# Attention with a mixture of experts: VectorE's norm statistics and expert choice move to other steps

## The reference

```
x = x + Attention(layernorm(x), ctx, ctx, mask)     16 heads of 64
    scores = q k^T + mask;  softmax;  probs v;  Wo
x = x + Experts(layernorm(x))
    s = sigmoid(xt gate^T);  the 4 largest of s + gate_b among 16 experts
    w = s of these 4, over their sum, times 2.5
    sum over the chosen e of w_e * (silu(gate_e) * up_e) W2_e^T,  plus one shared expert
```

## Time and profile before

| | us |
|---|---|
| median of 3 runs | 2065.05 (2064.69 to 2066.23) |
| profiled execution | 2066.34 |
| its span | 2064.5 |
| first phase, to the last step's start on VectorE | 1537.4 |
| TensorE busy | 2008.0 |
| VectorE busy | 1862.0 |
| ScalarE busy | 1670.5 |
| GpSimd busy | 1534.7 |

### The profile page before, as it was taken

How to read it: one execution, slowest core, us unless ns; L and a number is a source line. 1 busy time by engine, 2 the same in 40 slices (tenths; PEclk the granted TensorE clock), 3 DMA queues, 4 the chain that set the end, 5 groups by cost and what they waited for, 6 DMA issues and landing times.

```text
span 2064.5 us, 57695 instructions
## 1 busy us (share of the span) xinstructions
PE 2008.0 (97%) x16164; PEld 1948.3 (94%) x16164; DVE 1862.0 (90%) x6114; ACT 1670.5 (81%) x4763; POOL 1534.7 (74%) x2586
## 2 busy tenths in 40 slices
PE   6999999999999999999999999999988999999997
PEld 6999999999999999999999999999988999999996
DVE  6999999999999999999999999999987678888767
ACT  6999888888888888888898888888886666665663
POOL 4555577888888797978888887879777566665636
PEclk9999999999999999999999999999999999999999
DMA  7777778887878777866666566666577799988977
GB/s 206 189 186 186 182 192 216 214 218 206 213 205 218 211 208 208 212 174 172 172 170 163 161 173 169 164 167 167 150 209 228 280 314 314 309 306 293 304 247 248
DMA packets 252737, 440.00 MB, mean 213 GB/s; under 512 B 35600, under 2 KB 145680, under 8 KB 252432
## 3 DMA queue, kind: packets, MB, share of 16 engines
q1 hardware_dynamic: 227856, 369.17, 63.8%
q0 software_dynamic: 24576, 67.14, 10.0%
HBM read 133.40 MB, written 135.00 MB: 130 GB/s over the span
## 4 chain that ended last, share of the span: by engine, by line
PE 71%; DVE 19%; issue 5%; ACT 3%; POOL 1%; DMA 1%; SPq 0%; DVEq 0%; POOLq 0%; ACTq 0%
PE pj L115 9%; PE pj L117 8%; PE pj L116 8%; PE pV L1024 7%; PE pT L1011 7%; DVE E L1252 5%; PE epG L115 4%; PE epG L117 4%; PE epG L116 4%; PE pS L1000 4%; PE pS L1001 4%; PE epT L1795 4%; DVE PT_lo L1271 3%; DVE att_sum L1262 2%; PE epY L115 2%
## 5 line engine op out<-in xcount | busy, mean ns | idle before, releaser
L897 POOL TENSOR_SCALAR E<-E,rinv 128x256 f32<-128x256 f32 x1024 | 480.8, 479 | 245.5 <-DVE rinv L1227 233.4
L1092 ACT ACTIVATE E<-E,negmax 128x256 f32<-128x256 f32 x1024 | 509.2, 503 | 3.1 <-DVE negmax L1252 1.6
L1252 DVE CUSTOM_DVE_ANT_0 E<-pS,m_in 128x256 f32<-128x256 f32 x1024 | 386.4, 414 | 15.8 <-PE pS L1001 13.5
L1271 DVE TENSOR_TENSOR PT_lo<-pT,PT_hi 128x512 fp32r<-128x512 f32 x512 | 350.4, 684 | 9.6 <-ACT PT_hi L1110 1.5
L1750 POOL DMA_INDIRECT block<-expert_rows,slot x256 | 245.2, 958 | 147.0 <-PE epY L117 93.8
L1110 ACT ACTIVATE PT_hi<-pT 128x512 fp32r<-128x512 f32 x512 | 304.6, 595 | 8.4 <-PE pT L1011 1.0
L1011 PE MATMUL pT<-ident,E 128*128 128x128 f32 x2048 | 306.7, 272 | 0.0
L1024 PE MATMUL pV<-PT_hi,V 128*128 128x256 f32 x1024 | 286.0, 301 | 5.5 <-DVE PT_lo L1271 5.5
L1000 PE MATMUL pS<-qk_st 128*128 128x256 f32 x1024 | 268.2, 284 | 7.1 <-DMA qk_st<-qk_sp 7.1
L1001 PE MATMUL pS<-qk_st,qk_sp 128*128 128x256 f32 x1024 | 267.5, 282 | 0.0
L1024 PE MATMUL pV<-PT_lo,V 128*128 128x256 f32 x1024 | 266.5, 282 | 0.0
(11 more groups left out here) (332 smaller groups left out, 6789.6 us busy)
## 6 DMA issues: line engine op xcount, KB each, us to landing
qk_st<-qk_sp SPq DMA_DIRECT2D x512, 192.0 KB, 3.0
qk_st<-qk_sp SPq DMA_DIRECT2D x512, 128.0 KB, 3.3
sorted_rows<-qk_st SPq DMA_DIRECT2D x144, 256.0 KB, 3.8
xg<-sorted_rows SPq DMA_DIRECT2D x72, 512.0 KB
expert_rows<-block SPq DMA_DIRECT2D x72, 512.0 KB
c_in<-in_ctxT SPq DMA_DIRECT2D x32, 256.0 KB, 3.8
m_in<-in_mask SPq DMA_DIRECT2D x32, 256.0 KB
xn_rows<-rows SPq DMA_DIRECT2D x31, 256.0 KB
```

What stands on the lines that cost most here:

```text
L897: last = pool.tensor_scalar(e[:, t, :], e[:, t, :], rinv[:, r, t:t + 1], 1.0, ALU.mult, ALU.mult)
L1092: last = act.activation(E[r][:, t, :], E[r][:, t, :], ACT.Exp, bias=negmax[:, r, t:t + 1], scale=-1.0, accum_out=rowsum[:, r, t:t + 1])
L1252: last = dve.tensor_tensor_reduce(out=E[r][:, t, :], in0=pS[g % 2][:, t, :], in1=m_in.tile(b)[:, t, :], scale=-1.0, scalar=BIG, op0=ALU.ad ...
L1271: dve.tensor_tensor(lo[:, :, :], pT[n % 2][:, :, :], f32(hi[:, :, :]), ALU.subtract).then_inc(s_ptlo, 1)
```

## The change

The statistics of the first norm of batch b + 2 run in steps 13 and 15 of batch b (before: those of batch b + 1 in steps 0 and 2); for batch 1 alone they stay in steps 0 and 2 of batch 0. Their aggregation moves from step 4 to step 1, again except for batch 1. GpSimd's `inverse_std` stays at step 4 and now has a constant of its own. The first statistics of the second norm move from step 10 to step 9. The sixteen parts of an expert choice get another table, which spreads over steps 10 to 35 instead of 10 to 24; the last set whose choice lies in this phase keeps the old one. No operation is added or taken away.

```diff
--- before.py
+++ after.py
@@ -446,20 +446,22 @@
     CM_STEP, CS_STEPS = 1, (3, 5)
 
 
-    BN_STEPS, AG_STEP, XN_STEPS, XT_STEP = (0, 2), 4, (8, 9), 10
+    BN_FIRST, AG_FIRST = (0, 2), 4
+    BN_STEPS, AG_STEP, RSTD_STEP, XN_STEPS, XT_STEP = (13, 15), 1, 4, (8, 9), 10
 
     V_STEPS = (12 - H, 13 - H, 4, 5)
 
     WO_STEPS = (15, H + 1, H + 7, H + 9)
 
-    BN2_STEPS, AG2_STEP, XN2_STEPS, XN_OUT_STEP, RT_STEP, LG_STEP, LT_STEP = (10, 11), 12, (13, 15), 4, 3, 6, 8
+    BN2_STEPS, AG2_STEP, XN2_STEPS, XN_OUT_STEP, RT_STEP, LG_STEP, LT_STEP = (9, 11), 12, (13, 15), 4, 3, 6, 8
     END_STEPS = 2
 
     router = shared.router
     SET_FROM = [(SET_BATCHES * s + SET_BATCHES + 1) * H + LT_STEP + 1 for s in range(SETS - 1)]
     RANK_STEP = 11
     RANKS_AT = [(SET_BATCHES * s + SET_BATCHES + 2) * H + RANK_STEP for s in range(EARLY_SETS)]
-    CHOICE_AT = {10: (0,), 11: (1,), 13: (2, 3), 14: (4,), 15: (5, 6), 17: (7, 8), 19: (11,), 21: (9,), 22: (10,), 23: (12, 13), 24: (14, 15)}
+    CHOICE_AT = {10: (0,), 13: (1,), 14: (2,), 15: (3, 4, 5), 21: (6, 7), 22: (8,), 23: (9,), 25: (10,), 29: (11,), 31: (12,), 33: (13, 14), 35: (15,)}
+    LAST_CHOICE_AT = {10: (0,), 11: (1,), 13: (2, 3), 14: (4,), 15: (5, 6), 17: (7, 8), 19: (11,), 21: (9,), 22: (10,), 23: (12, 13), 24: (14, 15)}
 
     def choice_start(s):
         return (SET_BATCHES * s + SET_BATCHES + 1) * H
@@ -900,7 +902,7 @@
                     split_context(b + 1)
                 if h == CS_STEPS[1] and b + 1 < B:
                     split_context_low(b + 1)
-                if h == AG_STEP and b + 1 < B:
+                if h == RSTD_STEP and b + 1 < B:
                     inverse_std(b + 1)
                 if h == AG2_STEP and 0 <= b - 1 < EARLY:
                     inverse_std2(b - 1)
@@ -1274,10 +1276,12 @@
                 for i in later_weights(g):
                     weight_lo(i)
                 if 0 <= g < G and b + 1 < B:
-                    if h in BN_STEPS:
-                        statistics(b + 1, BN_STEPS.index(h))
-                    if h == AG_STEP:
+                    if b == 0 and h in BN_FIRST:
+                        statistics(b + 1, BN_FIRST.index(h))
+                    if h == (AG_STEP if b else AG_FIRST):
                         aggregate(b + 1)
+                    if h in BN_STEPS and b + 2 < B:
+                        statistics(b + 2, BN_STEPS.index(h))
                     if h in XN_STEPS:
                         apply_norm(b + 1, XN_STEPS.index(h))
                 if 0 <= b - 1 < EARLY:
@@ -1300,7 +1304,7 @@
                         dve.tensor_tensor(shared.sw13[1][:, :, at], source[:, :, :], f32(shared.sw13[0][:, :, at]), ALU.subtract)
                     dve.tensor_tensor(shared.sw2[1], c_in.tiles[1][:, 0, :], f32(shared.sw2[0]), ALU.subtract).then_inc(shared.s_swlo, 1)
                 for t in range(SETS - 1):
-                    for k in CHOICE_AT.get(g - choice_start(t), ()):
+                    for k in (CHOICE_AT if t < SETS - 2 else LAST_CHOICE_AT).get(g - choice_start(t), ()):
                         router.choose(dve, t, k)
                 if g == TABLE_AT:
                     router.tabulate(dve, 0)
```

## The result

| | before | after |
|---|---|---|
| median, us (6 runs each) | 2065.64 (2062.69 to 2067.38) | 2072.07 (2069.42 to 2073.62) |
| profiled execution, its span | 2066.34, 2064.5 | 2072.11, 2070.3 |
| TensorE, first to last step's start | 1517.0 | 1526.1 |

The ratio is 1.0029, 95% interval 1.0019 to 1.0039: the change makes the kernel slower by 6.4 us, where 7 us faster was forecast. In the profiled executions the first phase has grown by 9.1 us; the part behind it is 3.0 shorter, in one execution of each, and is not explained here.

A forecast was written before the change was run, and what follows sets the result against it. TensorE was taken as the bound, now and then held by VectorE. Terms summed to -0.55 us a pair of batches, times 14: -7.7; with 0.5 for late transfers and the median 1.3 below the profiled run, 2058 us, range 2048 to 2067.

The forecast's parts named there:

- E3: Step 3 of an even batch: VectorE's lag behind TensorE at its start falls from 2.00 to 1.6 us.
- E2: Step 2 of an even batch: statistics leave, counted as -0.34 us of VectorE's lag.
- E4: Step 4 of an even batch: its k projection waits less, losing 0.5 of the 0.75 us it is too long.
- O4: Step 4 of an odd batch: grows by 0.1 us, between 0 and +0.3, from work added before it.
- E7: Step 7 of an even batch: output projection waits for later router copies, losing about 0.4 us.
- E6: Step 6 of an even batch: VectorE's lag at its start rises from 1.17 to 1.58 us.
- O13: Step 13 of an odd batch: its whole wait of 0.29 us goes, counted as -0.3.
- E12: Step 12 of an even batch: falls by 0.25 to 0.3 us, counted as -0.3.
- E11: Step 11 of an even batch: keeps its 0.27 us wait and grows by up to 0.1, counted as +0.05.
- E10: Step 10 of an even batch: VectorE's lag at its start comes out 0.1 us higher.
- (b): Rival: slower by the new wait in E7, 2070 us at 1.3 us there; chance 0.12.
- (a): Rival: the waits only move, gain under 0.3 us a pair, 2062 to 2067 us; chance 0.20.
- (d): Rival: the mask is cheap at E9, -3.7 us more, 2054 us; chance 0.05.
- E9: Step 9 of an even batch: gains statistics (+0.34 us) and mask (+0.42 us) in VectorE's lag.

The follow-up runs named there:

- choice_only: Kernel before with only the choice of experts moved to the new table, statistics in their old steps; ratio 0.9942 to the kernel before.
- short_stat2: Kernel before with the first norm's second statistics (step 2) taken over 16 columns instead of 256; ratio 0.9999 to the kernel before.
- stats_only: Kernel after with the choice table put back, so only the norm statistics move; ratio 1.0038 to the kernel before.
- before_late_att_hi: Kernel before with ScalarE's att_hi issued one step later, behind the next step's exponentials, VectorE untouched; ratio 1.0029 to the kernel before.

## Why the prediction was wrong

- **The step that failed first: "the wait appears when the lag at E3 is over 1.48. The same holds wherever a short step with two projections precedes: E3, O3".** This is VectorE's own path. It decides in the kernel before and in choice_only, but it isn't the only one, and in the kernel after it was not the one that ended last: the chain through ScalarE from step 2 wants a lag under 1.06 there. The lag at E3 came out at 1.50, better than the forecast 1.6, but the lag at E2 only fell from 1.51 to 1.34, and E4 gave 0.19 of its 0.5. The price per statistics, 0.34, was taken off for step 2, where all but 0.1 of it had been free (short_stat2).
- **O4, forecast +0.1, measured +0.57**, is the same error. VectorE's lag at O2 went from 0.68 to 1.51; the old 0.68 had left 0.4 of room. Judged at O3 (1.30 to 1.71) it would have been 0.2, inside the bounds given. O4's 3.73 had also been read as 0.23 of wait: it is the shortest step 4 of any kernel, so that O4, and as much of E4's 0.75, had nothing to give.
- **E1, +0.49, had no term.** Its statistics and choice operations were counted as a lag carried on to E3; that E1's second fill needs a bank that VectorE has to read out on the way, and has its own point at 1.80, was missed. The table alone stays under it (1.64, E1 3.53), the statistics alone pass it (2.15, 3.88), both together reach 2.29 (4.02).
- **O11, +0.16, had no term**: the second norm's statistics, from O10 to O9, raise the lag at O10 from 0.90 to 1.24. It is there in stats_only (2.26) and not in choice_only (2.09).
- **Right: E7** +0.36 for +0.4 (lag at E6 1.49 for 1.58), **O13** -0.30, **E12** -0.33 for -0.3, and the covers: no wait of TensorE for a transfer is in the list of waits.
- **The terms together.** Forecast -0.55 a pair. Against it stand E1 0.49, O4 0.47, E4 0.31 and O11 0.16, and in favour E11 0.16, E10 0.06, E7 0.04 and E12 0.03: +0.59, measured 95.60 - 94.99 = +0.61.
- **A slip in the bounds.** With E7 and O4 free the terms add up to -1.05 a pair, not -1.2; it had no effect on the outcome.
- **The rivals.** (b) gave 2070, near the measured time, but by E7, which cost what the forecast said; it was right by accident. (a), up to 2067, had waits only move; here the new ones cost more than what went. (d) had its operation right: the mask at E9 takes 165 ns (median) against 450, and the lag at E10 fell by 0.16 where +0.1 was forecast. That helped E11, but the one-hot that took its place in E6 takes 0.62 a pair where it had 0.43 in E1.
- The threshold for TensorE's waits was the reason that E1, O4 and O11 were not looked for: steps without a wait were read as steps with nothing near. Their room (0.30 at E1, 0.38 at O4) was never computed.

## What to carry to other kernels

Before work is moved in an engine's list, write for each step that now has no wait how much lateness it bears, by every release it depends on, and follow a release back through all engines and not only along the one that does the last part. An operation that stands beside such a chain is nearly free; taking it away wins nothing, and putting it down elsewhere can cost. Room is used up by sums: two moves that each fit may not fit together. When busy times and the list of waits disagree with the time, compare step lengths, and before a wait is said to have moved, compare the durations of the same operations in both kernels.

## What the runs showed of the hardware

A VectorE tensor_scalar of 128x256 in SBUF, 0.40 us alone, took 0.54 when GpSimd's tensor_tensor had begun 0.34 before it, and 0.95 (median over the pairs) when that began 0.05 behind it. Moving one ScalarE copy turned 0.95 back to 0.54 and won 0.40 us a pair. The Trainium skill, page SBUF — State Buffer, section Who interferes with whom, says that a tensor_scalar in a two-port mode and a GpSimd instruction shut each other out entirely, and that the order of issue decides who waits. The trace bears this out in the main. In both cases the norm ends 0.15 to 0.16 behind the end of att_lo, whenever it began, as if it had been shut out until 0.25 before that end (GpSimd's spans are rough). Where att_lo begins 0.12 to 0.13 behind the norm (O9 of before_late_att_hi), it is the other way round: the norm takes 0.41, and att_lo 0.88 for its usual 0.73. In the case of 0.05 the profile has the norm first and yet the norm is the longer one, so starts as close as that don't tell who was first. That this norm runs in a two-port mode is not shown: alone it is no faster than the 128x256 operations with two inputs (0.40 to 0.42).

Operations with two inputs in SBUF behave alike beside GpSimd's cT_lo in step E6. The one-hot ends 0.28 behind it, whether it takes 0.63 or 1.25, for 0.43 in E1; the mask in the kernel before ends 0.05 behind it and takes 0.39 to 0.52, for 0.17 in E9. So starting the one-hot 0.63 earlier, beside the same operation of GpSimd, won nothing. Not every neighbour does this: beside GpSimd's indirect copy to sorted_rows, which begins 0.23 before it, the norm of E9 takes 0.40.
